# Two-layer transformer kernel on one Trainium2 core: the second layer's opening in another order on VectorE, ScalarE and TensorE

## What is computed

```python
x = L0_attn_h_t                                   # (8, 1024, 128)
xn = _layernorm(x)
x = x + _L0_attn_ref(xn, ...) + _L0_ffn_ref(xn, ...)   # latent attention, top-2 experts
xn = _layernorm(x)
x = x + _L1_attn_ref(xn, ...) + _L1_ffn_ref(xn, ...)   # flow attention, top-4 experts

# _L1_attn_ref (flow attention), 16 heads of 8
qkv = x @ qkv_w.T + qkv_b
q, k = sigmoid(q), sigmoid(k)
sink_incoming   = 1 / sum((q + EPS) * (k.sum(tokens) + EPS))
source_outgoing = 1 / sum((k + EPS) * (q.sum(tokens) + EPS))
...                                               # conserved flows, softmax over heads
out = ((q * sink_incoming) @ (k.T @ v_comp)) * sink_allocation
out = out @ proj_w.T + proj_b

# _L1_ffn_ref, 8 experts of width 256, computed densely
logits = x @ router_weight.T + router_bias
combine = softmax over the 4 largest logits, 0 elsewhere
gate = min(gate, 7);  up = clip(up, -7, 7)
act = (up + 1) * gate * sigmoid(1.702 * gate)
y = sum over experts of combine * (act @ down_proj.T + down_bias)
```

## Time and profile before

| | |
|---|---|
| median of 3 runs | 2896.59 us (2896.01 to 2897.06) |
| the profiled execution | 2897.44 us |
| its span in the trace | 2895.7 us |
| TensorE busy | 2512.6 us, 87% |
| VectorE busy | 2187.3 us, 76% |
| ScalarE busy | 1440.4 us, 50% |
| GpSimd busy | 704.7 us, 24% |
| mean granted TensorE clock | 0.944 of full speed |

### The profile page before, as it was taken

The page is one execution under the profiler, slowest core; times in us unless marked ns, Lnnn a source line. Parts: engine busy times, 40 slices in busy tenths (PEclk is TensorE's granted clock), DMA queues, the critical chain, the costliest instruction groups (busy, mean ns, idle before and its releaser), DMA issues. The chain is left out here.

```text
span 2895.7 us, 67341 instructions
## 1 busy us (share of the span) xinstructions
PE 2512.6 (87%) x26720; PEld 1816.3 (63%) x26720; DVE 2187.3 (76%) x3781; ACT 1440.4 (50%) x2616; POOL 704.7 (24%) x593
## 2 busy tenths in 40 slices
PE   4898889988898888998889979898798997989979
PEld 2666557665576656765667656676566765666646
DVE  4857778678777787776977769768697585985868
ACT  2755237552466434664256632567336572265813
POOL 1220332204322042220512205112152021520125
PEclk8999999999999999999999989999899998999989
DMA  5110211102111021110211112010120101201012
GB/s 218 38 37 2 84 48 38 37 2 95 37 38 37 2 99 34 41 34 6 98 30 45 30 38 73 26 46 27 41 76 27 45 19 52 66 29 48 14 55 70
DMA packets 93371, 136.26 MB, mean 47 GB/s; under 512 B 10111, under 2 KB 55240, under 8 KB 92552
## 3 DMA queue, kind: packets, MB, share of 16 engines
q1 hardware_dynamic: 84872, 115.16, 12.2%
q0 software_dynamic: 8192, 16.79, 1.9%
HBM read 101.31 MB, written 30.61 MB: 46 GB/s over the span
## 5 line engine op out<-in xcount | busy, mean ns | idle before, releaser
L1025 DVE TENSOR_REDUCE neg_max<-ps 128x1 f32<-128x1024 f32 x512 | 622.8, 1216 | 51.0 <-PE ps L1454 39.7
L700 ACT ACTIVATE probs<-ps,neg_max 128x1024 f32<-128x1024 f32 x512 | 571.1, 1116 | 158.2 <-DVE neg_max L1025 156.7
L1454 PE MATMUL ps<-keys,q_parts 64*128 64x512 f32 x3072 | 523.5, 448 | 82.7 <-ACT probs L700 56.6
L1331 PE MATMUL ps<-q_parts,w_split 128*128 128x512 f32 x1536 | 458.7, 434 | 68.7 <-DVE ffn L1147 41.0
L1331 PEld LDWEIGHTS ps<-q_parts,w_split 128*128 128x128 f32 x1536 | 281.7, 190 | 220.1 <-DVE ffn L1143 119.1
L599 POOL TENSOR_TENSOR probs<-ffn,q_parts 128x512 f32<-128x512 f32 x208 | 291.5, 1404 | 490.8 <-DMA q_parts<-gate_rows 276.9
L1475 PEld LDWEIGHTS ps<-ident,probs 64*128 64x128 f32 x8192 | 348.1, 143 | 96.0 <-ACT probs L700 17.2
L1454 PEld LDWEIGHTS ps<-keys,q_parts 64*128 64x128 f32 x3072 | 265.4, 196 | 220.8 <-ACT probs L700 108.3
L754 ACT ACTIVATE ffn<-ffn 128x512 f32<-128x512 f32 x256 | 159.9, 630 | 462.2 <-DVE ffn L1143 461.5
L1033 DVE COPY probsT<-ps 128x512 f32<-128x512 f32 x512 | 348.1, 680 | 23.6 <-PE ps L1475 23.6
L1475 PE MATMUL ps<-ident,probs 64*128 64x64 f32 x8192 | 350.2, 227 | 16.2 <-ACT probsT L682 16.2
(11 more groups left out here) (213 smaller groups left out, 3320.0 us busy)
## 6 DMA issues: line engine op xcount, KB each, us to landing
w_split<-w_parts SPq DMA_DIRECT2D x132, 256.0 KB, 2.6
q_parts<-gate_rows SPq DMA_DIRECT2D x64, 512.0 KB, 4.4
y_rows<-probs SPq DMA_DIRECT2D x40, 256.0 KB, 2.2
x_in<-in_x SPq DMA_DIRECT2D x9, 512.0 KB, 4.1
w_parts<-q_parts SPq DMA_DIRECT2D x2, 2048.0 KB, 14.4
out<-x_mid SPq DMA_DIRECT2D x8, 512.0 KB, 3.2
ffn<-in_gate_up SPq DMA_DIRECT2D x1, 2048.0 KB, 8.9
probsT<-in_gate_up SPq DMA_DIRECT2D x1, 2048.0 KB, 13.2
```

The lines of the kernel that those rows point to most:

```text
L700: nc.scalar.activation(probs[:, t % 3, :], banks(2 * (t % 2)), ACT.Exp, bias=neg_max[:, t % 4:t % 4 + 1], accum_out=row_sum[:, g % 2, t % ...
L1025: nc.vector.tensor_reduce(neg_max[:, t % 4:t % 4 + 1], banks(2 * (t % 2)), X, ALU.max, negate=True).then_inc(max_ready.sem, 1)
L1331: mm = nc.tensor.matmul(ps[:, bank, :], w_split[:, f % CHUNK_SLOTS, h, k * P:(k + 1) * P], tokens[:, half], start=(part == 0), stop=(part ...
L1454: mm = nc.tensor.matmul(ps[:, 2 * (t % 2) + c, :], q_parts[rows, j, q, n * P:(n + 1) * P], keys[rows, k, :], start=(part == 0), stop=(part ...
```

## The change

The routing is no longer spread over the qkv additions. On VectorE, `split_low` and then the whole of `route_four` come first; then follow `limits(0)`, two additions, `limits(1)`, four additions, `limits(2)`, the product of unit 0 and the last two additions. TensorE does two qkv tiles, `gate_up(0)`, `gate_up(1)`, the transposes of the gates, `gate_up(2)`, four tiles, `gate_up(3)` and the last two tiles. On ScalarE the Tanh moves behind the Silus of units 0 to 2. The steps of the flow attention up to `FLOW_KV` come one or two units later; `FLOW_SUMS`, `FLOW_OUT`, `FLOW_HEADS` and `FLOW_PROJ` stay. The number of instructions on each engine is unchanged.

```diff
-NEXT_TRANSPOSE = 14
+NEXT_TRANSPOSE = 15
...
-FLOW_SIGMOID = 0
+FLOW_SIGMOID = 2
+SIGMOID_UNIT = 3
 FLOW_SUMS = 4
-FLOW_WEIGHTS = (3, 4, 5, 6, 7, 8)
+FLOW_WEIGHTS = (4, 5, 6, 7, 8, 9)
...
-FLOW_KV = 19
+FLOW_KV = 20
...
                 copy_gatesT(b)
-                act.wait_ge(z_ready.sem, z_ready.at(b, NT))
-                nc.scalar.activation(qkv[:, :, 0:2 * D], qkv[:, :, 0:2 * D], ACT.Tanh, scale=0.5
-                                     ).then_inc(sig_tanh.sem, 1)
                 for u in range(UNITS):
+                    if u == SIGMOID_UNIT:
+
+                        act.wait_ge(z_ready.sem, z_ready.at(b, NT))
+                        nc.scalar.activation(qkv[:, :, 0:2 * D], qkv[:, :, 0:2 * D], ACT.Tanh, scale=0.5
+                                             ).then_inc(sig_tanh.sem, 1)
...
-                route = route_four()
-                for n in range(NT):
-
-                    next(route, None)
-                    if n == 1:
-                        split_low()
+                def biased(n):
                     dve.wait_ge(qkv_mm.sem, qkv_mm.at(b, n + 1))
                     nc.vector.tensor_tensor(qkv[:, n, :], ps[:, 6 + n % 2, 0:3 * D], b_qkv[:, :], ALU.add
                                             ).then_inc(z_ready.sem, 1)
-                    if n >= NT - 3:
-                        limits(n - (NT - 3))
-                assert next(route, "end") == "end"
...
+                split_low()
+                for _ in route_four():
+                    pass
+                limits(0)
+                biased(0)
+                biased(1)
+                limits(1)
+                for n in range(2, 6):
+                    biased(n)
+                limits(2)
+                product(0)
+                for n in range(6, NT):
+                    biased(n)
...
-                for n in range(NT):
+                def qkv_tile(n):
...
-                    if 3 <= n < 3 + EARLY_UNITS:
-                        gate_up(n - 3)
+
+                qkv_tile(0)
+                qkv_tile(1)
+                gate_up(0)
+                gate_up(1)
                 gates_transpose(b)
+                gate_up(2)
+                for n in range(2, 6):
+                    qkv_tile(n)
+                gate_up(3)
+                for n in range(6, NT):
+                    qkv_tile(n)
```

More of the change, by code:

```diff
@@ L69 @@
 EARLY_UNITS = 4
-FLOW_SIGMOID = 0
+FLOW_SIGMOID = 2
+SIGMOID_UNIT = 3
 FLOW_SUMS = 4
-FLOW_WEIGHTS = (3, 4, 5, 6, 7, 8)
+FLOW_WEIGHTS = (4, 5, 6, 7, 8, 9)
 FLOW_BIAS = 22
-FLOW_SUMS2 = 11
-FLOW_CONSERVED = (10, 11, 12, 13)
-FLOW_ALLOC = 14
-FLOW_VALUES = 15
-FLOW_KV = 19
+FLOW_SUMS2 = 12
+FLOW_CONSERVED = (11, 12, 13, 14)
+FLOW_ALLOC = 15
+FLOW_VALUES = 16
+FLOW_KV = 20
 FLOW_OUT = 22
@@ L1158, in _, with product @@
                                             ).then_inc(z_ready.sem, 1)
-                    if n >= NT - 3:
-                        limits(n - (NT - 3))
-                assert next(route, "end") == "end"
+                def product(u):
+                    dve.wait_ge(up_lim.sem, up_lim.at(b, u + 1))
+                    dve.wait_ge(silu_done.sem, silu_done.at(b, u + 1))
+                    if u >= 3:
+                        dve.wait_ge(h_ready.sem, h_ready.at(b, u - 2))
+                    nc.vector.scalar_tensor_tensor(ffn_gu[:, u % 3, :], ffn_u[u % 3], 1.0 - LIMIT,
+                                                   ffn_s[:, u % 3, :], ALU.max, ALU.mult).then_inc(gu_done.sem, 1)
+                split_low()
[11 more added lines that the diff above has]
+                    biased(n)
                 def flow_products(x, total):
@@ L1241, in _ @@
                 for u in range(UNITS):
-                    f = u // HALVES
                     if u >= 2 and u + 1 < UNITS:
                         limits(u + 1)
-                    dve.wait_ge(up_lim.sem, up_lim.at(b, u + 1))
-                    dve.wait_ge(silu_done.sem, silu_done.at(b, u + 1))
-                    if u >= 3:
-                        dve.wait_ge(h_ready.sem, h_ready.at(b, u - 2))
-                    nc.vector.scalar_tensor_tensor(ffn_gu[:, u % 3, :], ffn_u[u % 3], 1.0 - LIMIT,
-                                                   ffn_s[:, u % 3, :], ALU.max, ALU.mult).then_inc(gu_done.sem, 1)
+                    if u >= 1:
+                        product(u)
                     flow_step(u)
```

## The result

| | before | changed |
|---|---|---|
| median of 4 runs | 2896.82 us (2896.01 to 2899.30) | 2818.89 us (2817.08 to 2820.89) |
| the profiled execution | 2897.44 us | 2820.42 us |
| its span | 2895.7 us | 2818.7 us |
| mean granted clock | 0.944 | 0.949 |

The ratio is 0.9727, with an interval of 0.9713 to 0.974: the changed kernel is 2.7% faster. The forecast was 2815 us, within 2798 to 2840.

A forecast was written before the change was run, and what follows sets the result against it. The chain routing, transposes, copy, DRAM, GpSimd, `down`, sums was taken to end last in each batch's opening. Winning 10.2 us a batch, 81 in eight, gave 2897.4 - 81 = 2816, so 2815 us as median, within 2798 to 2840.

The forecast's parts named there:

- The gates' way: Opening, from the logits' start: routing done at +5.1 us, gates' copy at +8.4, gate rows at GpSimd at +15.5.
- Were the chain through the gates not what ends last, 2897 would stay.: Rival for the opening: routing, transposes, rows and GpSimd do not end last, so nothing changes, 2897 us; chance 0.03.
- What is late next: Opening behind the early gates: Tanh at +18.8 us, sigmoids and first `down` both at +20.9, then the sums over tokens.
- The opening as a whole: Logits' start to first flow product's end: +29.7 us against 39.85 with 2.04 of added work, 10.2 a batch won.
- more is won: Rival: TensorE's clock stays at 2.4 GHz all opening from gate_up 0 on, 12 us a batch, about 2801; chance 0.10.
- was said of `FLOW_OUT`: TensorE at unit 22: this unmoved step has 3.8 us of room, 1.5 left after the shift, so it costs nothing.
- slower: Rival: the kv step comes too late, TensorE stands at unit 22's `FLOW_OUT`; loss 1.3 us a batch, 2907; chance 0.05.
- The sums: TensorE's sums over tokens behind the first `down`: 3.62 us at full clock, ending at +24.5 from the logits.
- The first flow product: VectorE behind the sums: waits for gate_up 5, limits 5 and product 4 end at +28.0, the 1.68 us step at +29.7.
- VectorE and GpSimd collide: Rival: products 1, 2 and sigmoids fall into GpSimd's first multiplies, 2 us a batch remain, 16 more, 2831; chance 0.12.
- The first layer is untouched.: Rest of the batch: the change does not touch the first layer; no time was charged for it.
- The flow steps one unit later: Flow step moved from unit 3 to 4: VectorE does limits 5 and product 4 first, waiting 3 us for gate_up 5.

## Why the prediction was right, and where it was not

The forecast was 10.2 us a batch, 81 in all, and 77 were measured on the profiled executions. The total is nearer than its parts, and that is in part luck. The opening gained 88 (terms too long by more than the collision cost), 3 more came behind it, and 13.5 were lost in a stage that was said to stay as it was.

**The gates' way: right, step by step.** In the first batch `gate_w` is done at +5.1 (expected +5.1), the copy starts at +7.8 (+8.4) and GpSimd at +14.7 (+15.5). In batches 2 to 6 the copy starts at +6.5 to +6.7 and GpSimd at +13.7. The wait that should go went in all eight.

**"Were the chain through the gates not what ends last, 2897 would stay."** The chain did end last, but with 1.5 us to spare, and the prediction did not price the one behind it. With the early gates alone GpSimd starts at +30.0, later than before. What it did see and name, the turns of the two engines, was the cause of both: the limits of three units moved give 38 us. Only the sum over the new order was made, and that one takes both chains into account, which is why it came out.

**What is late next: the right instructions, too late by 1.3 to 2.3 us.** Additions, Tanh, sigmoids and the first `down` were expected to meet at +20.9. In the first batch the sigmoids ended at +19.6 and `down` started at +17.9; in batches 2 to 6 the sigmoids ended at +18.6. Two terms of the sum were too long. The durations of TensorE's rows were added end to end, and a row overlaps the next: the four middle tiles, put at 3.2 us, were 2.56 ahead of the next gate_up (295.71 to 298.27). So TensorE came to gate_up 4 at +14.2 even in the first batch, where +16.3 was expected. The other is the clock, of which the next paragraph tells. That the Tanh's place matters (about 50 us) was in the working as the Silus that stand ahead of it, without a price of its own.

**The opening as a whole.** 302.5 - 230.4 = 72.1, and with 2.04 us more of VectorE's work behind the mark in each batch 88.4: 11.0 a batch, against 10.2, and near the rival *more is won*. What that rival said, that the clock stays high from gate_up 0 on, came about in five of the eight batches: there two gate_ups took 3.66 to 3.88 us, where full clock gives 1.85 each, and the first flow product ended at +28.3. In the first batch they took 4.95 and it ended at +30.8, in the last two 4.5 and 4.6, and +29.2 and +29.0. 91.1 in the whole units' part means that nothing was given back there, as was said of `FLOW_OUT`, and the rival *slower* did not come near.

**The sums: right in seven batches of eight.** 3.62 was taken from rows at full clock; they took 3.72 in seven and 5.21 in the first, at a granted 0.50 in their first 3 us.

**The first flow product: the place was right, the price not.** The step said that VectorE "must wait for gate_up 5" and that the step itself takes 1.68. It took 0.42 + 2.13 because of GpSimd, in each of the eight batches: 0.9 a batch that no term held. The rival *VectorE and GpSimd collide* looked for the collision at products 1 and 2 and the sigmoids. Product 1 took 1.14 instead of 0.68, and the sigmoids were not slowed (1.22), since they started first and GpSimd's multiply at 305.23 was the slower one. The rule of the Trainium skill (SBUF — State Buffer, "Who interferes with whom"), that the one that starts first has the port for its whole instruction, agrees with both: GpSimd started 0.23 us ahead of the flow product, which took 0.91 more.

**"The first layer is untouched."** Its instructions are; its time was not. The step that failed is that an untouched stage costs what it did: 13.5 us went there by TensorE's clock, 2.2 of them in the first batch, where nothing that was changed had run yet. Why the same rows of TensorE with the same 15 us ahead of them kept the clock in one kernel and not in the other stays open. What the runs settle is where it falls (behind the narrow matmuls of the latents and of the router), and that with another order of the same matmuls it held in every batch of the traces that have it.

**The flow steps one unit later** were charged with a wait but not weighed against staying. They cost 17.5 us in the units' part, 2.2 a batch, and are the part of this change that should not have been made.

## What to carry to other kernels

Where two in-order engines wait for each other in turns, look first for the one short operation that releases the other engine's next work and put it right behind its input; here that alone was nearly half of the gain (38 of 78 us). A chain that ends last should be shortened only after the one next to it is priced, since a part of an edit can be worth nothing, a loss or most of the gain, depending on whether the other parts are there (the Tanh's place: about 5 us or about 50). After a change compare the stages that were not touched as well: the granted clock can move in them. And read more than the first batch: here it was the one with the lower clock.

## What the runs showed of the hardware

The latents' and the router's matmuls and the queries behind them ran at a granted 1.00 or partly at the 1.2 GHz level, for 1.7 us a batch. In the first batch this happened (1.00 against 0.50) with nothing different executed ahead of it. With wide matmuls between the two narrow groups the window behind them was at 1.00, and the stage took 22.3 us.

A wait of TensorE in the opening is mostly paid twice, once for itself and once in colder matmuls behind it. Where TensorE stood 3.8 to 4.7 us ahead of the first `down` (before) the sums took 4.6 to 5.2 us, behind 3.75 us (the Tanh first) 5.1 to 6.1, behind 2.3 to 2.8 us (the rows held back) 4.4 to 5.6, and in the changed kernel, where it stood nowhere for more than 0.9 us behind the router, 3.72 in seven batches. The first batch of the changed kernel, with 5.21, shows that the sums can be at the lower clock without such a wait.

A VectorE product of two SBUF inputs took 2.13 us instead of 1.23 when GpSimd had begun its multiply 0.23 us earlier, and a GpSimd multiply took 2.18 instead of 1.3 when VectorE's sigmoids had begun 0.16 us earlier.
